# Joining two of the three products of a split-precision layer into one of 512 columns

## What is computed

```
dots  = einsum("bfd,bgd->bfg", bottom_output, bottom_output)
x     = concat([bottom_mlp_output, dots[:, tril_i, tril_j], 0], axis=1)   # 2048 x 480
for w, b in ((w0, b0), (w1, b1), (w2, b2), (w3, b3)):                     # 1024, 1024, 512, 256
    x = relu(x @ w.T + b)
y     = x @ w_out.T + b_out                                               # 2048 x 1
```

## Time and profile before

| | us |
|---|---|
| median of 3 runs | 519.2 (518.56 to 519.43) |
| profiled execution, its own time | 517.22 |
| its span, first to last instruction | 515.2 |
| TensorE busy | 492.1 (96%) |
| VectorE busy | 329.1 (64%) |
| ScalarE busy | 296.8 (58%) |
| GpSimd busy | 256.3 (50%) |

### The profile page before, as it was taken

How to read it: one execution, slowest core, us unless ns; L and a number is a source line. 1 busy time by engine, 2 the same in 40 slices (tenths; PEclk the granted TensorE clock), 3 DMA queues, 4 the chain that set the end, 5 groups by cost and what they waited for, 6 DMA issues and landing times.

```text
span 515.2 us, 13763 instructions
## 1 busy us (share of the span) xinstructions
PE 492.1 (96%) x4073; PEld 485.4 (94%) x4073; DVE 329.1 (64%) x756; ACT 296.8 (58%) x734; POOL 256.3 (50%) x467
## 2 busy tenths in 40 slices
PE   6887987999999999999999999999999999999996
PEld 5876977999999999999999999999999999999996
DVE  2775889677873798458873788467863897331101
ACT  3565777656773686547763687457762786333112
POOL 2710355525864287625764386536763486524221
PEclk9988999999999999999999999999999999999999
DMA  8987977753663676257653766357644752310000
GB/s 237 239 290 166 263 118 123 136 99 67 104 102 70 107 117 107 49 122 114 102 81 80 121 103 108 66 108 115 96 67 102 126 90 33 69 31 0 1 1 0
DMA packets 281055, 53.24 MB, mean 103 GB/s; under 512 B 265126, under 2 KB 279230, under 8 KB 281022
## 3 DMA queue, kind: packets, MB, share of 16 engines
q1 hardware_dynamic: 279090, 52.22, 53.4%
q10 hardware_dynamic: 1932, 0.61, 0.5%
HBM read 45.71 MB, written 7.09 MB: 102 GB/s over the span
## 4 chain that ended last, share of the span: by engine, by line
PE 79%; DVE 2%; issue 2%; ACT 1%; POOL 1%; ACTq 0%; DVEq 0%; POOLq 0%
PE acc L752 69%; PE gram_ps L714 8%; PE gram_ps L665 1%; DVE xt L950 1%; ACT parts L843 1%; ACT h_full L859 1%; PE side_ps L765 0%; POOL grams L596 0%; DVE parts L972 0%; PE side_ps L726 0%; POOL parts L589 0%; DVE low_t L983 0%; DVE raw L945 0%; ACT y_row L876 0%; DVE h_b L990 0%
## 5 line engine op out<-in xcount | busy, mean ns | idle before, releaser
L752 PE MATMUL acc<-h_a,w_hi 128*128 128x256 f32 x1152 | 223.1, 284 | 2.0 <-DVE h_a L990 1.0
L752 PEld LDWEIGHTS acc<-h_a,w_hi 128*128 128x128 f32 x1152 | 184.8, 191 | 3.5 <-ACT h_full L859 2.0
L859 ACT ACTIVATE h_full<-acc,small_t 128x256 f32<-128x256 f32 x175 | 82.9, 474 | 143.9 <-PE acc L752 141.0
L752 PE MATMUL acc<-h_a,w_lo 128*128 128x256 f32 x576 | 158.6, 282 | 0.0
L604 POOL TENSOR_TENSOR h_a<-h_full,h_a 128x256 fp32r<-128x256 f32 x96 | 72.4, 754 | 133.1 <-DVE h_a L990 133.1
L843 ACT ACTIVATE parts<-gram_ps 27x216 f32<-27x216 f32 x336 | 114.5, 341 | 39.3 <-PE gram_ps L714 28.2
L752 PEld LDWEIGHTS acc<-h_a,w_lo 128*128 128x128 f32 x576 | 110.2, 191 | 0.0
L752 PE MATMUL acc<-x,w_hi 128*128 128x256 f32 x504 | 100.8, 287 | 3.3 <-ACT x L869 3.3
L752 PE MATMUL acc<-h_b,w_hi 128*128 128x256 f32 x512 | 97.2, 285 | 0.0
L752 PEld LDWEIGHTS acc<-x,w_hi 128*128 128x128 f32 x504 | 82.7, 193 | 4.1 <-ACT x L869 3.8
L604 POOL TENSOR_TENSOR h_b<-h_full,h_b 128x256 fp32r<-128x256 f32 x64 | 47.3, 739 | 71.8 <-DVE h_b L990 71.8
(11 more groups left out here) (60 smaller groups left out, 436.4 us busy)
## 6 DMA issues: line engine op xcount, KB each, us to landing
rows<-in_r_bottom_output_dram SPq DMA_DIRECT2D x444, 64.0 KB, 2.0
blocks<-grams SPq DMA_DIRECT2D x30, 216.0 KB, 3.9
w_raw<-in_L_rec_w_dram SPq DMA_DIRECT2D x6, 1024.0 KB, 7.6
early_rows<-in_r_bottom_output_dram SPq DMA_DIRECT2D x12, 224.0 KB, 6.2
stage_pairs<-in_L_rec_w_dram SPq DMA_DIRECT2D x1, 1408.0 KB, 9.7
w_raw<-in_L_rec_w_dram SPq DMA_DIRECT2D x2, 512.0 KB, 9.4
mlp_rows<-r_bottom_mlp_output_dram SPq DMA_DIRECT2D x8, 128.0 KB, 2.2
pairs<-blocks SPq DMA_DIRECT2D x8, 126.0 KB
```

The source lines that it names most:

```text
L752: last = nc.tensor.matmul(acc_slot(c, slot), weight(wp, layer, m, k), in_tile(layer, k, xp), start=(k == 0 and n == 0), stop=(k == K_TILES ...
L859: nc.scalar.activation(h_full[:, slot % 2, :], acc_slot(c, slot), ACT.Relu, bias=small_t[:, slot:slot + 1]).then_inc(drained, 1)
```

## The change

From chunk 1 on, tiles 1 to 6 of layer 1 and tiles 1 and 2 of layer 2 (`WIDE`) are computed with two products for each inner tile instead of three. The first takes w_hi with the high and low columns side by side, 512 columns, and fills the whole bank: the left half gets w_hi x high, the right half w_hi x low. The second, w_lo x high with 256 columns, is added to the left half. The weight tile w_hi is loaded once instead of twice.

The two halves have to be added when the tile is drained. ScalarE writes the right half plus bias into `h_full` (Identity), VectorE adds the left half to it (`add_halves`), ScalarE applies Relu in place, and then everything goes on as before. There are two new semaphores, `low_moved` (ScalarE to VectorE) and `halves_added` (VectorE to ScalarE). `add_halves` stands in VectorE's order directly before `split_high` of the same tile. ScalarE waits inside `drain` until VectorE has added.

```diff
--- before.py
+++ after.py
@@ -73,6 +73,7 @@
 EARLY_XT = 2 * XT_RING
 EARLY_BY_ACT = [1] * (UNITS - 2) + [2] * 2
 QUADS_BY_ACT = 3
+WIDE = [(1, m) for m in range(1, 7)] + [(2, 1), (2, 2)]
 OUT_HOOK, EARLY_TILES = 2, 4
 
 
@@ -326,6 +327,8 @@
         pairs_done = sem("pairs_done")
         filled = sem("filled")
         drained = sem("drained")
+        low_moved = sem("low_moved")
+        halves_added = sem("halves_added")
         high_done = sem("high_done")
         split_done = sem("split_done")
         mlp_turned = sem("mlp_turned")
@@ -353,6 +356,10 @@
 
             return c * FIRST_SLOT[3] + slot + 1
 
+        def wide_count(c, layer, m):
+
+            return (c - 1) * len(WIDE) + WIDE.index((layer, m)) + 1
+
         def slot_count(c, slot):
 
             return c * SLOTS + slot + 1
@@ -360,8 +367,12 @@
         def acc_slot(c, slot):
             if isinstance(c, int) and c == 0 and slot == ACC_RING:
 
-                return side_ps[:, 0:CHUNK]
-            return acc[:, RING_OF[slot], 0:CHUNK]
+                return side_ps[:, :]
+            return acc[:, RING_OF[slot], :]
+
+        def is_wide(c, layer, m):
+
+            return (layer, m) in WIDE and not (isinstance(c, int) and c == 0)
 
         def turned_bank(u):
 
@@ -371,9 +382,9 @@
         mlp_bank = side_ps[:, 0:CHUNK]
         out_bank = side_ps[0:1, CHUNK:]
 
-        def in_tile(layer, k, part):
+        def in_tile(layer, k):
             src = x0 if layer == 0 else h_b if layer == 2 else h_a
-            return src[:, k, part, :]
+            return src[:, k]
 
         def weight(part, layer, m, k):
             t = TILE0[layer] + m * K_TILES[layer] + k
@@ -747,10 +758,17 @@
                     if layer > 0 and m == 0:
 
                         pe.wait_ge(split_done if 2 in parts else high_done, split_count(c, slot_of(layer - 1, k)))
-                    for n in parts:
-                        wp, xp = ((w_hi, 0), (w_lo, 0), (w_hi, 1))[n]
-                        last = nc.tensor.matmul(acc_slot(c, slot), weight(wp, layer, m, k), in_tile(layer, k, xp),
-                                                start=(k == 0 and n == 0), stop=(k == K_TILES[layer] - 1 and n == 2))
+                    found, src, ends = acc_slot(c, slot), in_tile(layer, k), k == K_TILES[layer] - 1
+                    if is_wide(c, layer, m):
+                        nc.tensor.matmul(found, weight(w_hi, layer, m, k), src.rearrange("p h n -> p (h n)"),
+                                         start=(k == 0), stop=False)
+                        last = nc.tensor.matmul(found[:, 0:CHUNK], weight(w_lo, layer, m, k), src[:, 0, :],
+                                                start=False, stop=ends)
+                    else:
+                        for n in parts:
+                            wp, xp = ((w_hi, 0), (w_lo, 0), (w_hi, 1))[n]
+                            last = nc.tensor.matmul(found[:, 0:CHUNK], weight(wp, layer, m, k), src[:, xp, :],
+                                                    start=(k == 0 and n == 0), stop=(ends and n == 2))
                 if k1 == K_TILES[layer] and 2 in parts:
                     last.then_inc(filled, 1)
 
@@ -856,8 +874,14 @@
                 elif not (isinstance(c, int) and c == 0):
 
                     act.wait_ge(weighed, 2 * c - 1 + slot)
-                nc.scalar.activation(h_full[:, slot % 2, :], acc_slot(c, slot), ACT.Relu,
-                                     bias=small_t[:, slot:slot + 1]).then_inc(drained, 1)
+                full, found, bias = h_full[:, slot % 2, :], acc_slot(c, slot), small_t[:, slot:slot + 1]
+                if is_wide(c, layer, m):
+
+                    nc.scalar.activation(full, found[:, CHUNK:], ACT.Identity, bias=bias).then_inc(low_moved, 1)
+                    act.wait_ge(halves_added, wide_count(c, layer, m))
+                    nc.scalar.activation(full, full, ACT.Relu).then_inc(drained, 1)
+                else:
+                    nc.scalar.activation(full, found[:, 0:CHUNK], ACT.Relu, bias=bias).then_inc(drained, 1)
 
             def mlp_hi(d):
                 act.wait_ge(mlp_turned, d + 1)
@@ -983,6 +1007,12 @@
                 nc.vector.transpose(low_t[:, u % 2].rearrange("p j g -> p (j g)"),
                                     parts[:, u % 2, 1].rearrange("p j g -> p (j g)")).then_inc(low_turned, 1)
 
+            def add_halves(c, layer, m):
+
+                full, found = h_full[:, slot_of(layer, m) % 2, :], acc_slot(c, slot_of(layer, m))
+                dve.wait_ge(low_moved, wide_count(c, layer, m))
+                nc.vector.tensor_tensor(full, found[:, 0:CHUNK], full, ALU.add).then_inc(halves_added, 1)
+
             def split_high(c, layer, m):
 
                 slot, h = slot_of(layer, m), h_b if layer == 1 else h_a
@@ -1023,6 +1053,8 @@
                     if step[0] == "mm":
                         _, layer, m, _, k1, parts = step
                         if k1 == K_TILES[layer] and 2 in parts:
+                            if is_wide(c, layer, m):
+                                add_halves(c, layer, m)
                             if layer < 3:
                                 split_high(c, layer, m)
                             else:
```

## The result

The changed kernel takes 533.1 us (median of 5 runs, 532.7 to 535.0), the kernel before 519.3 us in the same session: **ratio 1.029, interval 1.026 to 1.033**. It is slower by 13.7 us, where 4.5 us faster had been forecast. The profiled execution has a span of 531.0 us.

What follows compares the result with a forecast made beforehand. TensorE, busy 96%, was taken as the bound, time past 100 us being the sum of product start intervals. Profiled: 517.22 - 6.0 + 1.5 = 512.7 us; against the median, 519.2 - 4.5 = 514.7 us, range 510.5 to 521.0.

Steps and rivals of the forecast that it cites:

- The product: In wide tiles, a 512-column product was taken at 0.2267 us, 0.0133 us saved per pair.
- the 6.0 of the sum: TensorE's saving over all wide tiles: 448 pairs x 0.0133 = 6.0 us, bounds 0 and 11.9.
- Rival B: No extra at all: the 512-column product takes 0.213 to 0.216 us, a pair 0.333; 509 to 510.2 us; chance 0.12.
- the rule cited with it: Interval at full clock of N / 2.4 + about 2.5 ns, 215.7 ns at 512 columns; would save 10.9 us.
- The chain of a wide tile: Drain of a wide tile: Identity 0.475, add 0.425, Relu 0.406 us; the chain grows by 0.91 us.
- Place 1, the casts: Layer 1: VectorE's casts of tiles 1 to 4 come 0.9, 1.85, 2.0 and 1.85 us later.
- the lag goes in tiles 5 and 6: Layer 1: hooks get light after tile 4, so VectorE's lag of up to 2.0 us disappears.
- Place 1, who waits: Layer 1: TensorE's gram needs a late copy; it fits with some 0.2 us, so 0 lost, with little cover.
- Place 2: End of layer 2: TensorE's wait for the drain of (2, 3) grows 0.30 us per loop chunk, 1.5 us in five.
- slower still: The rest of the chances, 0.03: a whole-kernel time slower than all the named cases.
- D: VectorE becomes the bound in layer 1: chain grows 1.2 us, TensorE waits at grams; 516.5 to 521 us, chance 0.14.
- C: The extra is a price per column: 512 columns take 0.240 us, nothing saved, 1.5 lost; 520.7 us; chance 0.21.

Runs made afterwards that it cites:

- products_only: The changed kernel with its wide products but the old one-pass drain from the left half; ratio 0.989 to the kernel before, median 513.1 us.
- rows_first: The changed kernel with SyncE issuing four row loads before the gather of the pairs instead of after it; ratio 1.000 to the kernel before.
- layer1_to4: The changed kernel with only tiles 1 to 4 of layer 1 wide, loads in their old order; ratio 1.014 to the kernel before.
- vector_relu: The changed kernel with VectorE applying Relu after its add, ScalarE making one pass, row loads in old order; ratio 1.020 to the kernel before.

## Why the prediction was wrong

**The product: right in kind, a little large.** Products in the changed kernel, three pairs apart in chunk 6 and 13 pairs apart in the last chunk:

```profile
448.91 0.28 PE L765 MATMUL acc<-h_a,w_lo 128*128 128x256 f32 x1
...
449.95 0.28 PE L765 MATMUL acc<-h_a,w_lo 128*128 128x256 f32 x1
...
504.01 0.28 PE L765 MATMUL acc<-h_a,w_lo 128*128 128x256 f32 x1
...
508.61 0.28 PE L765 MATMUL acc<-h_a,w_lo 128*128 128x256 f32 x1
```

1.04 / 3 = 0.347 us for a pair in chunk 6 and 4.60 / 13 = 0.354 in the last chunk, against 0.360 before. The mean over all pairs that follow one another is 0.349 in the loop, where three narrow products took 0.359, and 0.354 in the last chunk: 0.006 to 0.010 saved, where 0.0133 was taken. Over 448 pairs the traces of `products_only` and of the kernel before give 4.2 us for the 6.0 of the sum. Rival B's 0.333 does not hold, and neither does the rule cited with it from the Trainium skill (TensorE: Matmul & The Clock Gate, Wait — 56ns, not 53.3ns?), 215.7 ns for 512 columns: the median here is 230 ns in the loop and 236 in the last chunk.

**The chain of a wide tile: right.** Its three steps take 0.476, 0.425 and 0.418 us, where 0.475, 0.425 and 0.406 had been taken:

```profile
L880 ACT ACTIVATE h_full<-acc,small_t x56: 474/476/478, 142.0 to 520.3; 128x256 f32<-128x256 f32 x56
...
L1014 DVE TENSOR_TENSOR h_full<-acc,h_full x56: 423/425/426, 142.5 to 520.8; 128x256 f32<-128x256 f32 x56
...
L882 ACT ACTIVATE h_full<-h_full x56: 417/418/421, 143.0 to 521.3; 128x256 f32<-128x256 f32 x56
```

**Place 1, the casts: right for tiles 1 to 4, wrong for tile 5.** VectorE's casts of tiles 1 to 5, after (chunk begins at 250.00):

```profile
265.31 0.30 DVE L1020 CAST h_b<-h_full 128x256 fp32r<-128x256 f32 x1 [0.48 <-ACT h_full L882]
...
270.35 0.30 DVE L1020 CAST h_b<-h_full 128x256 fp32r<-128x256 f32 x1 [0.49 <-ACT h_full L882]
...
273.51 0.29 DVE L1020 CAST h_b<-h_full 128x256 fp32r<-128x256 f32 x1 [0.48 <-ACT h_full L882]
...
276.67 0.30 DVE L1020 CAST h_b<-h_full 128x256 fp32r<-128x256 f32 x1 [0.48 <-ACT h_full L882]
...
281.66 0.29 DVE L1020 CAST h_b<-h_full 128x256 fp32r<-128x256 f32 x1 [0.48 <-ACT h_full L882]
```

Into the chunk that is 15.31, 20.35, 23.51, 26.67 and 31.66 us; before it was 14.47, 18.59, 21.55, 24.87 and 28.95. They are 0.84, 1.76, 1.96, 1.80 and 2.71 us late; 0.9, 1.85, 2.0 and 1.85 had been worked out for the first four. The sentence "the lag goes in tiles 5 and 6" was not worked out, and it is false: with no raw and no turn left, the copies and sums of the last units still pass from ScalarE to VectorE to GpSimd and back one after the other, and tile 5 adds its own 0.9.

**Place 1, who waits: the step that failed.** The prediction asked only which of TensorE's products waits for the late engines. It found the gram with 0.2 us to spare. In fact that gram came 0.2 us late (0.33 us after the product before it, where 0.12 was due), which cost 0.28 us per chunk with the slower gram products behind the gap:

```profile
278.70 0.28 PE L765 MATMUL acc<-h_a,w_lo 128*128 128x256 f32 x1
279.03 0.68 PE L725 MATMUL gram_ps<-xt 128*128 128x224 f32 x4
```

But this is the small part. The prediction did not follow the steps that moved with VectorE to the other queues. GpSimd's last sum was one of them; behind it stood, on SyncE, a spill, a wait for it to land, a gather, and then loads that have nothing to do with either. Their rows were used 3.65 us after they were issued, with nothing in hand. "Place 1: 0, with little cover" should have been 5 x about 2.2 us of waiting on TensorE, and the half clock on top. The Trainium skill (DMA: Bandwidth & Descriptors, Two DMAs through the same engine are not ordered) has the issuing engine wait on the first DMA's semaphore before it issues one that reads what the first wrote. This kernel does so, and the trace agrees: 6.7 us from spill to gather before and 6.8 after. Here that wait also held up the loads behind it, which read nothing of the spill: four of them moved in front of it took 10.8 us of waiting and the half clock away (`rows_first`).

**Place 2: right, a little small.** The gap from 296.98 to 297.91 is 0.93 us, where 0.48 had been: 0.44 more, 0.30 forecast. ScalarE's pass behind the step at 295.72 started at 296.31, 0.59 later and not 0.46. 2.2 us instead of 1.5.

**The rivals.** The result fell into the 0.03 kept for "slower still". D had the right engine and the right sign but the wrong way: 0.28 us per chunk at the grams, and a loss from a chain of 0.91 us, not 1.2, that came through the loads. C fell with `products_only`. A slip that decides nothing: B's upper end is 519.2 - 10.7 + 1.5 = 510.0, not 510.2.

With the terms as measured the sum is 519.3 - 4.2 + 10.8 + 2.2 + 4.4 + 1.4 + 0.4 = 534.3 us, or 533.0 with the 5.5 us that the ratio of `products_only` gives, against 533.1 measured.

## What to carry to other kernels

When a step on an in-order engine moves back, list everything that its results release on every other queue, the DMA-issuing one first, and look at what stands behind a wait there: a load with no part in the matter may be the one that comes late. A transfer that shows no wait is not a transfer with slack; measure how long before its use it is issued and how long it takes. And try the change's halves apart, since here one half was worth about 1%, and most of the price of the other was a matter of where four loads stood.

## What the runs showed of the hardware

A TensorE wait of about 2 us was enough, three times in five, for 3.4 us at half clock (granted clock 0.50) behind it. In the changed kernel gaps between starts of 2.60, 2.11 and 2.25 us were followed by such a stretch, others of 2.23 and 1.68 us were not. In `layer1_to4` one of 1.56 us was and one of 1.81 was not; in `vector_relu` one of 2.32 was and one of 2.78 was not. So the length of the gap alone does not decide it, and short waits have a price that varies from chunk to chunk, nothing or some 1.5 us.

A 512-column product with 4-byte operands took 0.230 us from start to start in the loop (median of 320) and 0.236 in the last chunk (median of 64), where no work is woven in; the 256-column product behind it took 0.117 instead of 0.120. Why the wide one is faster in the loop stays open.
